# A CIN and dense tower on one core: the second half of layer 1's groups joins the three-pass product, and ScalarE and VectorE trade one bank per chunk

## What is computed

```python
def _cin_forward(inputs, filters):
    x0 = inputs
    prev = inputs
    outs = []
    for W in filters:
        z = jnp.einsum('bhd,bmd->bhmd', x0, prev)
        b, h, m, d = z.shape
        z = z.reshape(b, h * m, d)
        cur = jnp.einsum('bpd,pn->bnd', z, W[0])
        cur = jax.nn.relu(cur)
        prev = cur
        outs.append(cur)
    result = jnp.concatenate(outs, axis=1)
    return jnp.sum(result, axis=-1)
...
z = z.reshape(z.shape[0], -1)
h = jnp.concatenate([z, dense_ctx], axis=1)
h = jnp.maximum(h @ W_top1 + b_top1, 0.0)
h = jnp.maximum(h @ W_top2 + b_top2, 0.0)
y = h @ W_top3
```

## Time and profile before, and how to read it

| | |
|---|---|
| median of the runs | 859.55 us (858.24, 860.85) |
| the profiled execution | 856.8 us |
| its span (first to last instruction) | 855.0 us |
| mean granted TensorE clock | 0.996 |
| chunks in three passes for groups 2 and 3 | 29 of 32 (3 to 31) |

### The profile page before, as it was taken

The page is one execution under the profiler, slowest core; times in us unless marked ns, Lnnn a source line. Parts: engine busy times, 40 slices in busy tenths (PEclk is TensorE's granted clock), DMA queues, the critical chain, the costliest instruction groups (busy, mean ns, idle before and its releaser), DMA issues.

```text
span 855.0 us, 13830 instructions
## 1 busy us (share of the span) xinstructions
PE 847.2 (99%) x3527; PEld 663.0 (78%) x3527; DVE 787.5 (92%) x2394; ACT 679.0 (79%) x2231; POOL 661.5 (77%) x677
## 2 busy tenths in 40 slices
PE   8999999999999999999999999999999999999998
PEld 3777887777787777778777778877777877777874
DVE  4889999999999999999999999999999999999992
ACT  3778888788888888888888888887888888888862
POOL 5567888888788887777887878888878898867680
PEclk9999999999999999999999999999999999999998
DMA  5888666687766668776667775666877676784430
GB/s 169 194 201 208 159 135 139 163 184 170 178 138 140 155 162 187 164 163 157 132 162 164 181 167 128 146 160 163 183 170 154 131 164 164 161 186 84 91 74 1
DMA packets 55093, 131.05 MB, mean 153 GB/s; under 512 B 8036, under 2 KB 19140, under 8 KB 55013
## 3 DMA queue, kind: packets, MB, share of 16 engines
q0 software_dynamic: 22384, 68.70, 43.5%
q1 hardware_dynamic: 31090, 58.79, 22.7%
q10 hardware_dynamic: 1539, 2.67, 1.0%
HBM read 59.35 MB, written 4.20 MB: 74 GB/s over the span
## 4 chain that ended last, share of the span: by engine, by line
PE 92%; DMA 4%; DVE 2%; POOL 1%; ACT 1%; issue 0%; SPq 0%; DVEq 0%; ACTq 0%; POOLq 0%
PE t_act L797 13%; PE t_act L799 13%; PE t_act L798 13%; PE t_dve L797 13%; PE t_dve L799 13%; PE t_dve L798 13%; PE acc L764 6%; PE acc L769 5%; DMA prod<-prod 2%; PE acc L773 1%; DMA x_rows<-emb 1%; DVE prod L575 1%; POOL prod L303 1%; DVE prod L586 0%; PE t_act L875 0%
## 5 line engine op out<-in xcount | busy, mean ns | idle before, releaser
L418 ACT ACTIVATE prod<-t_act,weigh 128x128 f32<-128x128 f32 x2048 | 575.5, 371 | 102.7 <-PE t_act L799 96.9
L575 DVE SCALAR_TENSOR_TENSOR prod<-t_dve,weigh,prod 128x128 f32<-128x128 f32 x1792 | 481.0, 342 | 8.5 <-PE t_dve L799 6.4
L303 POOL TENSOR_TENSOR prod<-prod 128x512 f32<-128x512 f32 x254 | 298.8, 1176 | 29.6 <-DMA prod<-prod 19.0
L797 PE MATMUL t_act<-w_hi,cur_hi 128*128 128x512 f32 x512 | 212.4, 415 | 0.0
L799 PE MATMUL t_act<-w_hi,cur_lo 128*128 128x512 f32 x512 | 199.8, 390 | 0.0
L798 PE MATMUL t_act<-w_lo,cur_hi 128*128 128x512 f32 x512 | 199.6, 390 | 0.0
L797 PE MATMUL t_dve<-w_hi,cur_hi 128*128 128x512 f32 x512 | 199.6, 390 | 0.0
L799 PE MATMUL t_dve<-w_hi,cur_lo 128*128 128x512 f32 x512 | 199.3, 389 | 0.0
L798 PE MATMUL t_dve<-w_lo,cur_hi 128*128 128x512 f32 x512 | 199.1, 389 | 0.0
L287 POOL DMA_DIRECT2D prod<-prod x127 | 119.8, 943 | 90.2 <-ACT prod L418 46.0
L268 POOL DMA_INDIRECT emb<-table_dram,all_ids x128 | 156.7, 1224 | 39.9 <-issue 31.7
(11 more groups left out here) (92 smaller groups left out, 566.5 us busy)
## 6 DMA issues: line engine op xcount, KB each, us to landing
prod<-prod POOLq DMA_DIRECT2D x127, 512.0 KB, 5.1
x_shift<-x_rows SPq DMA_DIRECT2D x62, 512.0 KB, 6.6
x_pair<-x_rows SPq DMA_DIRECT2D x94, 128.0 KB, 4.5
x_same<-x_rows SPq DMA_DIRECT2D x31, 256.0 KB, 3.3
x_rows<-emb SPq DMA_DIRECT2D x64, 64.0 KB
w_raw<-w_dram ACTq DMA_DIRECT2D x8, 256.0 KB, 4.2
emb<-table_dram,all_ids POOLq DMA_INDIRECT x128, 3.0
w_raw<-wt_dram SPq DMA_DIRECT2D x2, 512.0 KB, 7.5
```

The lines of the kernel that those rows point to most:

```text
L303: nc.gpsimd.tensor_tensor(src[:, dst, :], src[:, dst, :], src[:, other, :], ALU.add).then_inc(folded, 1)
L418: last = nc.scalar.activation(prod[i][:, HEADS * a + j, :], t_act[n % ARING][:, j * MAPS:(j + 1) * MAPS], ACT.Copy, scale=weigh[p][:, i, h ...
L575: nc.vector.scalar_tensor_tensor(dst, src, w, dst, ALU.mult, ALU.add).then_inc(added, 1)
L797: nc.tensor.matmul(bank[:, :], cur_hi[p][:, cols], w_hi[:, w], start=True, stop=False)
```

## The change

Groups 0 and 1 of chunks 3 to 31 are multiplied in three passes as well. ACT gets a second rounding (`round_first`), DVE two more subtractions (`lower_first`). `round_last` moves from behind ACT's third tile to behind the fourth. In the fourth tile of chunks 1 to 30 the banks are split five to ACT and three to DVE (`FULL`). A tile with five A banks has 20 places in `prod`, so its fold is a DMA of 128x1280, additions of 128x640, 128x256 and 128x128, and the one into `side`. To make room in SBUF, four small tensors of the top now lie in others' memory, and the waits for D buffers in the top are counted anew.

```diff
-ORDER = [FULL if False else EVEN for tile in range(CHUNKS * TILES)]
+ORDER = [FULL if tile % TILES == TILES - 1 and tile < (CHUNKS - 1) * TILES and tile >= TILES else EVEN for tile in range(CHUNKS * TILES)]
...
-        z_hi = sb("z_hi", [128, SPLIT, COLS], f32r)
-        z_lo = sb("z_lo", [128, SPLIT, COLS], f32r)
+        z_hi = sb("z_hi", [128, GROUPS, COLS], f32r)
+        z_lo = sb("z_lo", [128, GROUPS, COLS], f32r)
...
+            def round_first(c, p):
+
+                act.wait_ge(z_ready, c * 3 + 1)
+                act.wait_ge(layer1_half, c - 1)
+                nc.scalar.activation(z_hi[:, 0:WHOLE, :], z[p][:, 0:WHOLE, :], ACT.Copy).then_inc(first_rounded, 1)
...
-                    if i == 2 and not ((c == 0 or c + 2 >= CHUNKS)):
+                    if i == 2 and 0 < c < CHUNKS - 2:
+                        round_first(c + 2, p)
+                    if i == 3 and 0 < c < CHUNKS - 2:
                         round_last(c + 2, p)
...
+            def lower_first(c, p):
+                dve.wait_ge(first_rounded, c - LEAD + 1)
+                for g in range(WHOLE):
+                    nc.vector.tensor_tensor(z_lo[:, g, :], z[p][:, g, :], z_hi[:, g, :].bitcast(fp32),
+                                            ALU.subtract).then_inc(first_lo_ready, 1)
...
-            nc.vector.tensor_copy(v_hi[:, :, :], v[:, WHOLE:GROUPS, :]).then_inc(v_ready, 1)
+            nc.vector.tensor_copy(v_hi[:, :, :], v[:, :, :]).then_inc(v_ready, 1)
...
                 if more2:
                     products(c + 2, p, 1)
+                    if c > 0:
+                        lower_first(c + 2, p)
...
-                    if g < WHOLE or g < GROUPS and c <= 2:
+                    if g < GROUPS and c < LEAD:
...
-                        nc.tensor.matmul(acc1[:, :], v[:, g, :], z[p][:, g, :], start=g == 0, stop=False)
+                        last = nc.tensor.matmul(acc1[:, :], v[:, g, :], z[p][:, g, :], start=g == 0, stop=False)
+                        if g == WHOLE - 1:
+                            last.then_inc(layer1_half, 1)
...
+                        if g < WHOLE:
+                            pe.wait_ge(first_lo_ready, (c - LEAD) * WHOLE + g + 1)
+                        else:
+                            pe.wait_ge(z_lo_ready, (c - LEAD) * WHOLE + g - WHOLE + 1)
+                        nc.tensor.matmul(acc1[:, :], v_hi[:, g, :], z_hi[:, g, :], start=g == 0, stop=False)
+                        nc.tensor.matmul(acc1[:, :], v_lo[:, g, :], z_hi[:, g, :], start=False, stop=False)
+                        last = nc.tensor.matmul(acc1[:, :], v_hi[:, g, :], z_lo[:, g, :], start=False, stop=False)
...
-                pe.wait_ge(added, (D_UPTO[-1] - DRING + f + 1) * HEADS)
+                last = D_UPTO[-1] - 1
+                pe.wait_ge(added, (last - (last - f) % DRING + 1) * HEADS)
```

More of the change, by code:

```diff
@@ L15 @@
 GROUPS = 4
[L16 to L17 removed]
+WHOLE = GROUPS // 2
 BANK = 512
@@ L74, in dlrm_tower @@
         v = sb("v", [128, GROUPS, MAPS])
-        v_hi = sb("v_hi", [128, SPLIT, MAPS], f32r)
-        v_lo = sb("v_lo", [128, SPLIT, MAPS], f32r)
+        v_hi = sb("v_hi", [128, GROUPS, MAPS], f32r)
+        v_lo = sb("v_lo", [128, GROUPS, MAPS], f32r)
         v_last = sb("v_last", [3 * FIELDS, MAPS])
@@ L109, in dlrm_tower @@
         apart2 = x_shift[0].rearrange("x h (i c q) -> x h i c q", i=TILES, q=QUARTERS)
+        room = 2 * TOP1 + T1 * TOP2
+        ctx_sb = w_raw[0:CTX, room:room + BATCH]
+        wt1_ctx = w_raw[0:CTX, room + BATCH:room + BATCH + TOP1]
         h2 = w_raw[:, 2 * TOP1 + T1 * TOP2:2 * TOP1 + T1 * TOP2 + T2 * BATCH].rearrange("n (f b) -> n f b", f=T2)
-        pool1_hi, pool1_lo = (sb(f"pool1_{half}", [128, BATCH], f32r)[:, :] for half in ("hi", "lo"))
+        pool1_hi, pool1_lo = z_hi[:, 0, :], z_lo[:, 0, :]
         h1 = z[0]
@@ L394, in round_pair @@
                 act.wait_ge(layer1_done, c)
[L395 removed]
+                nc.scalar.activation(z_hi[:, WHOLE:GROUPS, :], z[p][:, WHOLE:GROUPS, :], ACT.Copy).then_inc(pair_rounded, 1)
             def relu2(c, p):
@@ L763, in layer1 @@
                             pe.wait_ge(z_ready, c * 3 + 3)
-                        nc.tensor.matmul(acc1[:, :], v[:, g, :], z[p][:, g, :], start=g == 0, stop=False)
+                        last = nc.tensor.matmul(acc1[:, :], v[:, g, :], z[p][:, g, :], start=g == 0, stop=False)
+                        if g == WHOLE - 1:
+                            last.then_inc(layer1_half, 1)
                     elif g < GROUPS:
-                        k = g - WHOLE
-                        pe.wait_ge(z_lo_ready, (c - 3) * SPLIT + k + 1)
-                        for weights, rows in ((v_hi, z_hi), (v_lo, z_hi), (v_hi, z_lo)):
-                            nc.tensor.matmul(acc1[:, :], weights[:, k, :], rows[:, k, :], start=False, stop=False)
+                        if g < WHOLE:
[5 more added lines that the diff above has]
+                        last = nc.tensor.matmul(acc1[:, :], v_hi[:, g, :], z_lo[:, g, :], start=False, stop=False)
+                        if g == WHOLE - 1:
+                            last.then_inc(layer1_half, 1)
                     else:
```

14 lines of the change are left out of this document (5 added, 9 removed).

## The result

The changed kernel takes 883.02 us (882.13 and 883.92) against 859.55: 1.0277 times as long, with a 95% interval of 1.0222 to 1.0331. It is slower. The forecast was 849, the range ended at 874. The profiled execution took 882.13, with a span of 880.3.

What follows compares the result with a forecast made beforehand. PE was taken as the bound, 92% of the chain; its saving of -11.6 us and +1.5 for ACT's buffers made -10.1, from the median 859.55 to 849 us, all other terms 0 or hidden. The range was 845 to 874.

Steps and rivals of the forecast that it cites:

- PE's saving: Six fp32r matmuls replace four fp32 records: 0.40 us a chunk, cadence 25.14 to 24.74, -11.6 us over 29 chunks.
- ACT's dead heats: PE's fourth A bank and next tile's first are due just as ACT frees buffers: 0.05 us a chunk, +1.5 us.
- The walk: Instruction times in a chunk, from ACT's `relu2` at T+6.00 through `round_first` and five banks, against PE's need for A banks.
- T: Start of the first matmul of a chunk's third tile, 416.70 in the prediction's walk; later times count from it.
- Rival C: The A buffers hold PE: both dead heats cost 0.1 us each a chunk, 854 us; chance 0.08.
- DVE's own work: Two added subtractions less four multiply-adds: +0.17 us a chunk, within the 0.95 us wait before the third tile.
- +0.9 a chunk, where POOL idles 2.48 us before `halve` 3: hidden: POOL's longer fourth-tile fold, 128x640 and an added 128x128, costs +0.9 us a chunk, covered by idle time.
- The meeting of DVE and POOL, taken as 0: Behind DVE's fourth tile, POOL's fold could block an added subtraction: between 0 and 1.6 us a chunk, taken as 0.
- POOL waits and DVE loses nothing: The fold behind `halve` 3 starts 0.2 to 0.3 us after DVE's second subtraction has started, so POOL is blocked.
- Rival A: DVE becomes the bound, blocked at the second subtraction behind its fourth tile: cadence 25.3 to 25.9, 865 to 883 us; chance 0.20.
- rival B: A third to a half of the chunks are blocked by DVE-POOL meetings, paying 0.6 to 1.2 us: 857 us; chance 0.14.
- perhaps 1.0: DVE's room per chunk in us, counting its waits for banks; 0.38 by the wait before the third tile alone.

Runs made afterwards that it cites:

- `e3_narrow_folds`: The changed kernel with POOL's fold additions over 16 of 128 columns of each field, the rest of the fold left out; 845.31 us.
- `e1_even_banks`: The changed kernel with four banks each for ACT and DVE in every tile, three passes for all four groups kept; 866.06 us.
- `e15_narrow_fourth_only`: The changed kernel with only the 640-column addition of the fourth tile's fold done over 16 of each 128 columns; 848.49 us.
- `e4_subs_earlier`: The changed kernel with the two added subtractions ahead of DVE's fourth tile instead of behind the product after it; 877.31 us.
- `e10_quarter_fourth`: The changed kernel with a second accumulating DMA doing the fourth tile's 640-column addition, the fold following one tile later; 865.93 us.
- `e13_one_group_lo_psum`: The changed kernel with four banks each in all tiles, only group 1 added to the three passes, and `cur_lo` taken from PSUM; 852.02 us.

## Why the prediction was wrong

**PE's saving: right.** PE in the changed kernel, the first matmul of the new block of six and the one behind it:

```profile
106.87 0.39 PE L789 MATMUL acc<-z_hi,v_hi 128*128 128x512 f32 x1
...
108.23 0.39 PE L821 MATMUL t_act<-w_hi,cur_hi 128*128 128x512 f32 x1
```

1.36 us for six, as worked out. With 24.81 and 24.78 in the first steps, and 24.79 in `e3_narrow_folds`, a chunk without meetings stands 0.05 above the 24.74: the saving of 0.40, and ACT's dead heats at 0.05. In `e1_even_banks`, without the fifth A bank, two of the first chunks take 24.74 and 24.73.

**ACT: right.** The walk had `relu2` at T+6.00, `round_first` at T+6.52 and the five banks from T+7.47. ACT in the second steady chunk (T = 115.26; the last row shows 18 of the tile's 20 instructions):

```profile
121.26 0.65 ACT L409 ACTIVATE cur<-side 128x512 f32<-128x512 f32 x1
121.78 1.08 ACT L397 ACTIVATE z_hi<-z 128x1024 fp32r<-128x1024 f32 x1
122.73 4.76 ACT L425 ACTIVATE prod<-t_act,weigh 128x128 f32<-128x128 f32 x18
```

That is T+6.00, T+6.52 and T+7.47. Rival C has no part in the result: PE's weight loads for A banks waited for ACT 4.0 us in the whole run.

**DVE's own work: right.** The product came at T+11.88 (forecast T+11.75) and the subtractions at T+13.01 (T+12.88). The added lines have a median of 0.68.

**POOL, "+0.9 a chunk, where POOL idles 2.48 us before `halve` 3: hidden": this is the step that failed.** The size was right (1.83 for 128x640 in place of 1.56, and 0.74 for the added 128x128, 1.0 together). The cover was taken from the wrong place. The long fold runs at the start of a chunk, and the 2.48 us stand behind the third tile's fold. In between lie two folds with only 0.58 us of idle time between them, and they move with POOL: the last addition into `side` slid from T+10.48 to T+11.82, onto DVE's product and the two new subtractions, lost 2.34 us there, and the 2.48 were gone in the first steady chunk. The sum also had no term for the bigger DMA: it landed after 9.2 us in place of 5.1, and the long fold waited for it 0.7 us a chunk (21.2 in all). Cutting the 128x640 addition alone, with that DMA in place, brought 34.5 of 37.7 us.

**The meeting of DVE and POOL, taken as 0: wrong with it.** It was 2.15 us a chunk, against 1.03 of room. The walk looked at one place, the fold behind `halve` 3, and took `halve` 3 at its old distance from ACT's end. The first three steady chunks of `e15_narrow_fourth_only` show that this picture holds when POOL is in time. The sentence "POOL waits and DVE loses nothing" holds for the instruction and not for the chunk: in the changed kernel DVE waited at the products, `z_last` and `cur_lo`, two-input instructions that were there before.

**Rival A was the case, with another place.** DVE as the bound, a block of 1.34 to 1.6 a time, a cadence "25.3 to 25.9" and 865 to 883: the cadence was 26.08 and the time lies at its upper end. The place was not the second subtraction but `cur_lo` and `z_last`, and at the start it was POOL that fell 1.3 us back, not DVE 0.25 against ACT. The remark that POOL's longer fold moves other meetings too was the cause, and the prediction had put it last. It had 0.20 of the chance. That the two engines keep one phase from chunk to chunk was counted against rival A, and rival B said that they met in 2 of 29 chunks only. Both came from looking for the big losses of 1.6: ten steady chunks of the kernel before had a `cur_lo` of 0.94 to 1.21, hidden by DVE's idle time. The prediction's guess at that room, "perhaps 1.0", was good; it priced too few instructions against it.

**What stays open.** In what order the meetings build up isn't settled: `e4_subs_earlier` is as slow although `side` isn't held there, and `e15_narrow_fourth_only` is fast although it is. What a late POOL costs depends on which of DVE's instructions its folds meet, and no run delayed POOL alone. Why the 640 KB DMA takes 1.8 times as long as that of 512 KB was not tried. The chunk of 30.88 us in `e10_quarter_fourth` was seen in one profile only. And the 3 us that narrow folds gain in the kernel before, outside its steady chunks, were not followed.

## What to carry to other kernels

Idle time covers added work only if it stands behind that work and ahead of the first other engine it can disturb; walk the late engine forward instruction by instruction until it meets the first idle time, and ask at each step what it now runs beside. Where two engines block each other's instructions, a steady phase can break: price the loss for all two-input instructions of the chunk, not only for the ones added, and set it against the idle time that the engine has left. Here 0.9 us a chunk stayed nearly hidden (`e15_narrow_fourth_only`), and 2.15 cost the kernel 2.8%. A step that is half as big (`e13_one_group_lo_psum`) can stay inside that room and win where the whole one loses.
